# Attention taken two chunks of keys at a time, with the output projection's half tile in three parts in the bank of the sums

## The reference

```python
def attn(x, ...):                      # x: (16, 2048, 1024), 16 heads of 64
    q = x @ q_w.T + q_b                # 2048 queries
    xd = conv1d(x, conv_w, stride 2) + conv_b
    k, v = xd @ k_w.T + k_b, xd @ v_w.T + v_b      # 1024 keys
    att = softmax(q k^T / 8)
    return (att v) @ out_w.T + out_b
def ffn(x, ...):                       # 4 experts, top 1
    e = argmax(x @ W_router)
    h = gelu(x @ W1[e] + b1[e])
    return layernorm(h @ Wo + bo + x) * gamma + beta
xn = layernorm(x)
out = x + attn(xn) + ffn(xn)
```

## Time and profile before

| what | us |
|---|---|
| median of 3 runs (slowest core) | 1967.33 (1964.52 to 1977.75) |
| the profiled execution's own time | 1971.07 |
| its span on the slowest core (core 3) | 1969.5 |
| spans of the 8 cores | 1947.0 to 1969.5 |
| PE / ACT / DVE busy on core 3 | 1828.8 / 895.2 / 934.0 |

### The profile page before, as it was taken

The page is one execution under the profiler, slowest core; times in us unless marked ns, Lnnn a source line. Parts: engine busy times, 40 slices in busy tenths (PEclk is TensorE's granted clock), DMA queues, the critical chain, the costliest instruction groups (busy, mean ns, idle before and its releaser), DMA issues.

```text
span 1969.5 us, 37041 instructions; the slowest of 8 cores (1947.0 to 1969.5 us)
## 1 busy us (share of the span) xinstructions
PE 1828.8 (93%) x12540; PEld 1004.3 (51%) x12540; DVE 934.0 (47%) x1257; ACT 895.2 (45%) x1381; POOL 298.3 (15%) x357
## 2 busy tenths in 40 slices
PE   3588999998999999887899999999999999999995
PEld 1245222232554222222566666766666676666663
DVE  3354689856563888774132233413333323332225
ACT  2244988887455977775122222322222322222221
POOL 3122001001230110011001111101111111101111
PEclk9799999999999999998999999999999999999998
DMA  7759989984686999954756566856555776556551
GB/s 172 182 150 122 181 159 172 162 156 144 183 174 138 141 167 169 166 184 156 260 195 216 203 213 215 266 207 218 211 204 186 249 263 212 183 188 208 203 197 72
DMA packets 89171, 366.69 MB, mean 186 GB/s; under 512 B 11792, under 2 KB 11936, under 8 KB 68000
## 3 DMA queue, kind: packets, MB, share of 16 engines
q1 hardware_dynamic: 50112, 252.06, 38.8%
q0 software_dynamic: 38880, 112.27, 29.7%
...
## 4 chain that ended last, share of the span: by engine, by line
PE 73%; DMA 10%; DVE 6%; ACT 6%; issue 3%; POOL 0%; SPq 0%; DVEq 0%; ACTq 0%; POOLq 0%
PE ff_py L981 25%; PE ff_pu L946 25%; ACT pbuf L556 5%; DMA xa_d<-stg 4%; PE ps_a L505 4%; PE ps_s L543 4%; PE ps_a L569 4%; PE ps_q L367 3%; DMA row<-x 3%; DVE rc L581 3%; PE ps_q L395 2%; PE ps_m L574 2%; PE ps_q L381 2%; DMA xn_d<-row 2%; DMA stg<-x 1%
## 5 line engine op out<-in xcount | busy, mean ns | idle before, releaser
L960 ACT ACTIVATE ff_it<-ff_pu,b1t 128x256 bf16<-128x256 f32 (+1 forms) x608 | 244.3, 453 | 729.6 <-PE ff_pu L946 729.6
L556 ACT ACTIVATE pbuf<-ps_s 128x1024 bf16<-128x1024 f32 x512 | 477.3, 1061 | 116.8 <-PE ps_s L543 99.4
L946 PE MATMUL ff_pu<-ff_xg,ff_w 128*128 128x256 bf16 (+1 forms) x4864 | 516.4, 265 | 1.1 <-DVE ff_xg L930 1.1
L981 PE MATMUL ff_py<-ff_wo,ff_it 128*128 128x512 bf16 x2240 | 510.7, 381 | 3.8 <-DVE stg L511 3.8
L946 PEld LDWEIGHTS ff_pu<-ff_xg,ff_w 128*128 128x128 bf16 x4864 | 444.9, 98 | 73.4 <-issue 1.3
L981 PEld LDWEIGHTS ff_py<-ff_wo,ff_it 128*128 128x128 bf16 x2240 | 218.7, 98 | 238.2 <-issue 8.1
L581 DVE RECIPROCAL rc<-ps_m 128x512 f32<-128x512 f32 x64 | 214.7, 3355 | 44.9 <-PE ps_m L574 44.2
L569 PE MATMUL ps_a<-pbuf,v_sb 128*64 128x512 bf16 x1024 | 209.1, 404 | 5.8 <-DVE masks_all L464 4.8
L543 PE MATMUL ps_s<-qT,kT 64*128 64x512 bf16 x1024 | 201.3, 384 | 11.9 <-ACT pbuf L556 9.7
L574 PE MATMUL ps_m<-pbuf,ones 128*64 128x512 bf16 x1024 | 197.7, 381 | 0.0
L930 DVE COPY ff_xg<-ff_pt 128x1024 bf16<-128x1024 bf16 x35 | 24.2, 691 | 348.0 <-PE ff_pt L923 348.0
...
## 6 DMA issues: line engine op xcount, KB each, us to landing
ff_w<-scrW SPq DMA_DIRECT2D x152, 1024.0 KB
...
```

The lines of the kernel that those rows point to most:

```text
L556: e_at[g] = op("scalar", lambda s: s.activation(pbuf[g % 4][:, :], ps_s[g % 2][:, :], AF.Exp, scale=0.125), w)
L946: E.emit("tensor", lambda t, r_=r, q_=q, ic_=ic, c=cc, j_=j, sl=k % NW1SLOT: t.matmul(pu[r_][:, q_, 0:n], w1[:, sl, c * 512 + ic_ * 128:c ...
L960: E.emit("scalar", lambda s, r_=r, q_=q, ic_=ic, i_=i, j_=j, k_=k: s.activation(it[:, k_ % 3, ic_, 0:n], pu[r_][:, q_, 0:n], AF.Gelu, bias ...
L981: E.emit("tensor", lambda t, a_=a, o=oh, ic_=ic, i_=i, k_=k: t.matmul(py[:, 2 * a_ + o, :], it[:, k_ % 3, ic_, a_ * 128:(a_ + 1) * 128], w ...
```

## The change

The loop of `attention` now takes two chunks at a time. Both exponentials and both scores (each scores still waiting for the exponential two chunks earlier) come first, then the side work of both chunks, then values of both chunks, then sums of both. In the last two chunks of a pair the sums come ahead of the values, so that the reciprocal can begin earlier. `out_unit` becomes `out_part`: three matmuls after the sums of kc 2 and 3, three after those of kc 4 and 5, and the last two after the scores that are issued in kc 6 and 7. It accumulates in `ps_m`, the bank of the sums of the other parity, and so waits for the reciprocal of the pair before, where it waited for the product before. The side work that needs a bank takes `ps_a` in turn; the two routing steps on TensorE are held to kc 6. `flush_stores` moves from kc 1 to kc 0. The tail of the output projection (after the last pair) uses `ps_m` too.

```diff
-    def out_unit(b, qb, u, si):
+    def out_part(b, qb, u, si, ocs):
-        for oc in range(CC):
+        at = 5 + 2 * si
+        for oc in ocs:
             m = op("tensor", lambda t, o=oc: t.matmul(
-                ps_a[si][:, :], otp[qb % 2][:, o, tt * 128:(tt + 1) * 128],
+                ps_m[si][:, :], otp[qb % 2][:, o, tt * 128:(tt + 1) * 128],
...
-                ([otp_at[(b, qb)], W["o"]] + K.bank[4 + 2 * si]) if oc == 0 else [], inc=oc == CC - 1)
+                ([otp_at[(b, qb)], W["o"]] + K.bank[at]) if oc == 0 else [], inc=oc == CC - 1)
+        if ocs[-1] < CC - 1:
+            return
...
+        def divide(P, m_sum, m_val):
+            m = op("vector", lambda v: v.reciprocal(rc[:, :], ps_m[si][:, :]), [m_sum] + K.rc)
+            K.bank[5 + 2 * si] = [m]
+            w = [m, m_val]
...
-        for g in range(NG):
+        for g in range(0, NG, 2):
...
-            expo(g)
-            if g + 2 < NG:
-                scores(g + 2)
-            if kc == 5 and qb >= 1:
-                out_unit(b, qb - 1, hp, (P + 1) % 2)
-            if kc == 1:
+            for q in (g, g + 1):
+                expo(q)
+                if q + 2 < NG:
+                    scores(q + 2)
+            if kc == 6 and qb >= 1:
+                out_part(b, qb - 1, hp, 1 - si, (6, 7))
+            if kc == 0:
                 flush_stores()
             side(P, kc)
-            values(g)
+            side(P, kc + 1)
+            if kc == NKC - 2:
+                sums(g)
+                m_sum = sums(g + 1)
+                values(g)
+                m = values(g + 1)
+                divide(P, m_sum, m)
+            else:
+                values(g)
+                values(g + 1)
+                sums(g)
+                m = sums(g + 1)
+            pv_at[g] = pv_at[g + 1] = pv_last[b] = m
+            if kc in (2, 4) and qb >= 1:
+                out_part(b, qb - 1, hp, 1 - si, (0, 1, 2) if kc == 2 else (3, 4, 5))
...
-            a_transpose(gt - 1, 5 + 2 * ((P + 1) % 2))
+            a_transpose(gt - 1, 4 + 2 * ((P + 1) % 2))
...
-            if kc in ((2, 6) if "texp" in M else (2, 4, 6)):
+            on_pe = "sum" not in M or M.get("left") == 2
+            if kc in ((6,) if on_pe else (2, 6) if "texp" in M else (2, 4, 6)):
```

More of the change, by code:

```diff
@@ L244, in build_nc @@
     ps_m = [bank(f"ps_m{i}", [128, 512], F32, 5 + 2 * i) for i in range(2)]
-    ps_t = {i: bank(f"ps_t{i}", [128, CC, 128], BF16, i) for i in (5, 7)}
+    ps_t = {i: bank(f"ps_t{i}", [128, CC, 128], BF16, i) for i in range(4, 8)}
     m_const = None
@@ L511, in out_unit @@
         m = op("vector", lambda v: v.tensor_tensor(
-            stg[s_][:, oh * 512:(oh + 1) * 512], ps_a[si][:, :], stg[s_][:, oh * 512:(oh + 1) * 512], op=ALU.add),
+            stg[s_][:, oh * 512:(oh + 1) * 512], ps_m[si][:, :], stg[s_][:, oh * 512:(oh + 1) * 512], op=ALU.add),
             [m, mx])
-        K.bank[4 + 2 * si] = [m]
+        K.bank[at] = [m]
         if oh == 1:
@@ L560, in values @@
             P, kc = divmod(g, NKC)
-            qb, hp = divmod(P, HP)
+            hp = P % HP
             si = P % 2
@@ L564, in values @@
             if kc == 0:
-                w = w + K.bank[4 + 2 * si] + K.bank[5 + 2 * si]
+                w = w + K.bank[4 + 2 * si]
             if g < NKC:
@@ L568, in values, with sums @@
             for h in range(2):
-                op("tensor", lambda t, h_=h: t.matmul(
+                m = op("tensor", lambda t, h_=h: t.matmul(
                     ps_a[si][64 * h_:64 * (h_ + 1), :], v_sb[:, kc, (2 * hp + h_) * 64:(2 * hp + h_ + 1) * 64],
                     pbuf[g % 4][:, h_ * 512:(h_ + 1) * 512], start=(kc == 0), stop=(kc == NKC - 1)),
-                    w if h == 0 else [], inc=False)
+                    w if h == 0 else [], inc=h == 1)
+            return m
+        def sums(g):
+            P, kc = divmod(g, NKC)
+            si = P % 2
+            w = [e_at[g], m_ones] + (K.bank[5 + 2 * si] if kc == 0 else [])
             for h in range(2):
@@ L576, in values @@
                     pbuf[g % 4][:, h_ * 512:(h_ + 1) * 512], start=(kc == 0), stop=(kc == NKC - 1)),
-                    inc=h == 1)
-            pv_at[g] = m
-            pv_last[b] = m
-            if kc == NKC - 1:
-                m = op("vector", lambda v: v.reciprocal(rc[:, :], ps_m[si][:, :]), [m] + K.rc)
-                K.bank[5 + 2 * si] = [m]
-                w = [m]
-                if qb >= 2:
-                    w.append(op_last[(b, qb - 2)])
-                elif b:
-                    w = w + [op_last[(b - 1, NQB - 2 + qb)], kv_last["v", b * NQB + NQB - 1]]
-                else:
-                    w.append(kv_last["v", b * NQB + NQB - 1])
-                m = op("vector", lambda v: v.tensor_tensor(
-                    otp[qb % 2][:, hp, :], ps_a[si][:, :], rc[:, :], op=ALU.mult), w)
-                K.bank[4 + 2 * si] = [m]
-                otp_at[(b, qb)] = m
-                K.rc = [m]
+                    w if h == 0 else [], inc=h == 1)
+            return m
+        def divide(P, m_sum, m_val):
+            qb, hp = divmod(P, HP)
+            si = P % 2
+            m = op("vector", lambda v: v.reciprocal(rc[:, :], ps_m[si][:, :]), [m_sum] + K.rc)
+            K.bank[5 + 2 * si] = [m]
+            w = [m, m_val]
+            if qb >= 2:
+                w.append(op_last[(b, qb - 2)])
+            elif b:
+                w = w + [op_last[(b - 1, NQB - 2 + qb)], kv_last["v", b * NQB + NQB - 1]]
+            else:
+                w.append(kv_last["v", b * NQB + NQB - 1])
+            m = op("vector", lambda v: v.tensor_tensor(
+                otp[qb % 2][:, hp, :], ps_a[si][:, :], rc[:, :], op=ALU.mult), w)
+            K.bank[4 + 2 * si] = [m]
+            otp_at[(b, qb)] = m
+            K.rc = [m]
         scores(0)
         scores(1)
-        for g in range(NG):
+        for g in range(0, NG, 2):
             P, kc = divmod(g, NKC)
             qb, hp = divmod(P, HP)
+            si = P % 2
             if kc == 0 and 2 <= P <= 26 - 3 * b or kc == 4 and P % 4 == 0 and 4 <= P <= 24 - 4 * b:
@@ L619, in unit @@
         def unit(u):
-            out_unit(b, NQB - 1, u, u % 2)
+            out_part(b, NQB - 1, u, u % 2, range(CC))
             flush_stores()
@@ L1173, in side1 @@
     def side1(P, kc):
-        K.at = 5 + 2 * ((P + 1) % 2)
+        K.at = 4 + 2 * ((P + 1) % 2)
         if kc == 0 and P in (10, 18, 26):
@@ L1184, in side1 @@
         elif "rt" not in M:
-            if kc in ((2, 6) if "texp" in M else (2, 4, 6)):
+            on_pe = "sum" not in M or M.get("left") == 2
+            if kc in ((6,) if on_pe else (2, 6) if "texp" in M else (2, 4, 6)):
                 step = next(rt)
+                M["sum"] = True
+                if step == "left":
+                    M["left"] = M.get("left", 0) + 1
                 if "texp" in M and M["texp"] < 4:
```

1 line of the change is left out of this document (added).

## The result

| what | before | after |
|---|---|---|
| median of all 4 runs each, us | 1966.24 | 2009.77 |
| the runs, us | 1964.52 to 1977.75 | 1996.62, 2005.16, 2014.38, 2213.28 |
| ratio with 95% interval | | 1.0198 [1.0158, 1.0239] |
| profiled execution's own time / span | 1971.07 / 1969.5 | 2014.38 / 2012.8 |

In some executions of any of these kernels the cores of one die run at a lower granted clock and take some per cent longer (the 2213.28 here); the medians in us are over all runs, and the ratios compare the others alone, for which the median after is 2005.16.

The account below looks back on a forecast made before the run. Bounds before: ScalarE in pairs 0 to 7, VectorE in 8 to 20, TensorE in 22 to 26. Terms summed to +30.7, taking 1971.07 to 2001.8; that execution stood 3.7 above the median, hence 1998 us, range 1970 to 2013.

Parts of the forecast that it names:

- ScalarE's loop: Pairs 0 to 7: exponential, late scores, early scores, exponential; 7.90 us a pair instead of 7.37, +8.5 in all.
- VectorE's loop: Pairs 8 to 20: reciprocal, projection's first part, last part, addition, reciprocal; 10.08 us a pair instead of 9.20, +22.9.
- entering it: Start of VectorE's loop: half a microsecond more in each batch, +1.
- all from pair 21 on (0.9 + 2 - 3.7): Pairs 22 to 26 +0.9, transposes, normalisation and routing pairs +2, `rt_pq` no longer waiting for the reciprocal -3.7.
- last reciprocal earlier: Last step of attention: sums ahead of values start the last reciprocal 0.45 us earlier, -0.9 for two batches.
- rival C: Waits of some 1 us a pair make TensorE's clock fall in 26 pairs, +1.5 each: 2037 us; chance 5%.
- From pair 22: Pairs 22 to 26: TensorE's saving is spent waiting before late scores; 9.18 us a pair against 9.03, +0.15.
- A: TensorE's work decides: pairs with TensorE as bound fall from 9.03 to 8.15 us, total 1943; chance 10%.
- B: Only ScalarE's loop costs, VectorE's loop stays open: pairs 8 to 20 keep 9.20, +6.8, total 1974 us; chance 15%.

Follow-up runs that it names:

- e9: Two kernels: the changed kernel with the sums of two, or of four, of eight chunks left out in pairs 0 to 7; 2003.18 and 2011.9 us.
- e6: Changed kernel with third product at kc 5, projection in two parts of four matmuls, pairs 0 to 7 by single chunks; 1966.15 us, ratio 0.9991.
- e3: Changed kernel with the third product of pairs 8 to 20 at kc 5 instead of kc 6, ahead of the addition; 1974.17 us, ratio 1.0037.
- e4: Changed kernel with the projection's parts back in the bank of the values, side work in that of the sums; 2050.16 us, ratio 1.0422.
- e1: Changed kernel with chunks one by one again, projection still in three parts in the bank of the sums; 1975.5 us, ratio 1.0032.
- e7: Kernel before with banks exchanged as in the change: single chunks, whole projection at its old place, routing steps at kc 6; 1963.1 us, ratio 0.9971.
- e8: e7 up to pair 21, with the changed kernel's order (two chunks, projection in three parts) from pair 22 on; 1967.5 us, ratio 0.9995.
- e2: Changed kernel with the projection whole again behind the scores issued in kc 4, and the old banks; 1990.32 us, ratio 1.0110.

## Why the prediction was right

Step by step, measured on core 0 (both batches), against the forecast:

| term | forecast | measured |
|---|---|---|
| ScalarE's loop, pairs 0 to 7 | +8.5 | 4.2 + 1.6 = +5.8 |
| VectorE's loop and entering it, pairs 8 to 20 | +23.9 | 18.0 + 12.9 = +30.9 |
| all from pair 21 on (0.9 + 2 - 3.7) | -0.8 | -0.6 - 2.4 = -3.0 |
| last reciprocal earlier | -0.9 | -1.0 |
| sum | +30.7 | +32.7 |

The mechanism came as forecast: two loops, of the length that was worked out, and a third stage in which what TensorE saves is spent in waits. That the sums lie only 2.0 apart is in part luck, since the terms miss in both directions (-2.7, +7.0, -2.2, -0.1). The stretches hold 7 and 14 turns, the forecast counts 8 and 13 pairs.

**ScalarE's loop.** The pair was forecast at 7.90 and came at 7.88 in the steady turns of batch 0. e9 showed that TensorE's work is in it, e6 that single chunks take it away. The term was mis-sized in batch 1: I took both batches alike. There VectorE, behind after pair 2 (a turn of 11.0), sets the pace of pairs 3 to 7 at 7.2 in both kernels, and the longer loop is hidden: +1.6 instead of +4.2.

**VectorE's loop.** 10.08 forecast, 10.06 measured; TensorE to the first part 0.15, the addition at 4.62 to 4.65 after the reciprocal's end against 4.65 forecast and VectorE idle in front of it. e3 and e4 moved it as a loop moves, and e1's turn is the same sum without the product. In batch 0 the loop alone is 14 x (10.06 - 9.20) = 12.0, against a forecast of 13 x 0.88 = 11.4 and 0.5 for entering. The other 6.0 of the 18.0 are mainly two things that I had priced too low. One is entering, 2.3 in the batch: in the first pair of a block of queries (8 and 16) the first part reads `otp` of the whole block before, so it waits for the product behind the reciprocal (the 347.82 row), and pair 8 takes 11.21 instead of 10.06. I had said half a microsecond a batch, and forgot the second block. The other is rival C in small, 2.9: behind waits of 1.19 and 1.98 TensorE ran at 1.2 GHz (the 335.17 row, and from 349 to 352 us), and two turns took 11.51 and 12.65 instead of 10.06 and 11.21. I had given that 5% as a case for every pair; it came in a few, and belonged into the likeliest case as a surcharge. It is also what differs between cores: core 4 has none of it in batch 0 and loses 15.1 there, and 16.0 in batch 1. The last 0.7 are two turns of 10.41, in which the addition starts 1.14 instead of 0.78 after the last two matmuls; what holds it is open.

**From pair 22.** 9.18 forecast; 9.17 measured in the steady turns, but 9.40 in the mean of the four, since pairs 23 and 24 took longer (9.54 and 9.72), for which I had no term. `rt_pq` lost its wait as forecast, and e7 shows that the gain of the new banks with the routing steps at kc 6 is larger than the 3.7 of the wait: 7.3 us on core 0 in batch 1, since the half clock behind the wait goes too. The changed kernel shows less of it since the pairing costs there (e8).

**The last reciprocal.** -1.0 on core 0 but +0.7 on core 4: the stretch holds the whole next stage and scatters by more than the term. It stays open.

**The slowest core.** By the ratio 39 us were lost, by core 0's stretches 32.7, by core 4's 36.1. The profiled execution adds the 0.81 clock of cores 2 and 3, which began ahead of the loops, and the runs 1996.62 to 2014.38 lie 18 us apart. What sets such a clock stays open.

**Rivals.** A (TensorE's work decides) is refuted by pairs 22 to 26, 9.17 and more, and not 8.15. The Trainium skill (TensorEngine Tiling, Key Properties) says that a change of mode drains TensorE. The rows agree, with about 0.1 us more from couple to couple across a change, but it did not decide: e2 has fewer changes of mode than the kernel before and is 1.1% slower. B (the loop stays open) is what e3 is, and its 1974 is what e3 measures: 1974.17. To that closeness it is luck, since by the stretches e3 is 2.5 us above the kernel before on core 0 and 7.4 on core 4, against 6.8 in B.
